# Layer 1 attention: gathers indexed from the slot table, later loads, and another order for the first tile

## The reference

```
x = x + tanh(g_xattn[0]) * L0_attention(layernorm(x), ctx)
x = x + tanh(g_ffn[0])   * L0_experts(layernorm(x))        # top 2 of 8
x = x + tanh(g_xattn[1]) * L1_attention(layernorm(x), ctx) # 16 heads, softmax over 77 keys
x = x + tanh(g_ffn[1])   * L1_ffn(layernorm(x))            # quantised weights and activations
```

## Time and profile before

| | us |
|---|---|
| median of 3 runs | 1357.1 (1356.96 to 1358.56) |
| the profiled execution, its own time | 1351.81 |
| its span, first to last instruction | 1350.1 |
| of it, layer 1 attention (901.36 to 1199.62) | 298 |
| mean granted TensorE clock | 0.949 |
| busy: TensorE / VectorE / ScalarE / GpSimd | 1194.5 / 982.7 / 811.0 / 549.5 |

### The profile page before, as it was taken

How to read it: one execution, slowest core, us unless ns; L and a number is a source line. 1 busy time by engine, 2 the same in 40 slices (tenths; PEclk the granted TensorE clock), 3 DMA queues, 4 the chain that set the end, 5 groups by cost and what they waited for, 6 DMA issues and landing times. The chain is left out here.

```text
span 1350.1 us, 26442 instructions
## 1 busy us (share of the span) xinstructions
PE 1194.5 (88%) x8487; PEld 899.4 (67%) x8533; DVE 982.7 (73%) x2135; ACT 811.0 (60%) x2405; POOL 549.5 (41%) x594
## 2 busy tenths in 40 slices
PE   4989898996986499999999999957999999959898
PEld 3878797884543277777777777734777777735475
DVE  4998889793554166666666667736888888859898
ACT  2555545452654256665566665516777777829898
POOL 4666757573204222221111112116888888710000
PEclk9999999998887599999999999988999999979999
DMA  3223233223774325333333332236224242100033
GB/s 116 64 94 94 72 94 93 70 79 95 254 217 117 134 59 138 112 114 118 115 112 118 122 115 95 69 112 180 63 64 139 64 139 64 41 12 1 32 98 122
DMA packets 124158, 135.30 MB, mean 100 GB/s; under 512 B 13838, under 2 KB 108740, under 8 KB 123908
## 3 DMA queue, kind: packets, MB, share of 16 engines
q1 hardware_dynamic: 116577, 114.81, 27.6%
q0 software_dynamic: 6816, 18.62, 5.1%
q10 hardware_dynamic: 642, 0.33, 0.1%
HBM read 84.43 MB, written 49.29 MB: 99 GB/s over the span
## 5 line engine op out<-in xcount | busy, mean ns | idle before, releaser
L1403 ACT ACTIVATE exp_h<-exp_ps_h,exp_b_now 128x256 f32<-128x256 f32 x312 | 128.8, 463 | 159.4 <-PE exp_ps_h L1343 156.2
L1343 PE MATMUL exp_ps_h<-exp_xhi,exp_w_now 128*128 128x256 bf16 x1248 | 214.8, 276 | 4.4 <-DVE exp_xlo L1433 4.4
L1788 ACT ACTIVATE a_z<-a_ps_sc,a_nmx 128x77 f32<-128x77 f32 x512 | 159.2, 368 | 56.2 <-DVE a_nmx L1889 56.2
L1343 PE MATMUL exp_ps_h<-exp_xlo,exp_w_now 128*128 128x256 bf16 x624 | 172.1, 276 | 0.0
L1510 DVE TENSOR_TENSOR exp_hlo<-exp_h,exp_hhi 128x512 bf16<-128x512 f32 x156 | 106.7, 691 | 80.4 <-ACT exp_hhi L1407 77.1
L1355 PE MATMUL exp_ps_y<-moe_w2s,exp_hhi 128*128 x585 | 139.2, 379 | 2.0
L1343 PEld LDWEIGHTS exp_ps_h<-exp_xhi,exp_w_now 128*128 128x128 bf16 x1248 | 123.5, 99 | 20.6 <-issue 5.0
L1788 ACT ACTIVATION_READ_ACCUMULATOR a_z<-a_ps_sc,a_nmx 128x1 f32 x512 | 127.9, 250 | 0.0
L1311 POOL COPY exp_at_now<-all_token_of 128x2 int32<-128x2 int32 x39 | 8.4, 216 | 288.7 <-PE exp_ps_x L1330 273.2
L1755 PE MATMUL a_ps_o<-a_v_now,a_phi 128*128 128x256 bf16 (+1 forms) x640 | 106.5, 272 | 15.4 <-DVE a_plo L1878 15.4
L1407 ACT ACTIVATE exp_hhi<-exp_h 128x512 bf16<-128x512 f32 x156 | 98.3, 630 | 4.9
(11 more groups left out here) (245 smaller groups left out, 2959.7 us busy)
## 6 DMA issues: line engine op xcount, KB each, us to landing
a_stage<-in_L_ffn_W_dram SPq DMA_DIRECT2D x64, 256.0 KB
y_slots<-exp_y SPq DMA_DIRECT2D x78, 128.0 KB
fold_k<-route_kst SPq DMA_DIRECT2D x16, 308.0 KB, 4.3
fold_v<-route_vst SPq DMA_DIRECT2D x16, 308.0 KB
exp_job_in<-fold_k SPq DMA_DIRECT2D x14, 352.0 KB, 3.4
exp_job_in<-fold_v SPq DMA_DIRECT2D x14, 352.0 KB, 3.3
a_x<-in_x_dram SPq DMA_DIRECT2D x32, 128.0 KB, 2.4
x<-a_xo SPq DMA_DIRECT2D x32, 128.0 KB, 1.7
```

What stands on the lines that cost most here:

```text
L1343: mm = pe.matmul(ps_h[:, i, f % 2 * SLOT_T:(f % 2 + 1) * SLOT_T], w1_now[:, v, k, hl, f * P:(f + 1) * P], xx[:, k, :], start=(q == 0), sto ...
L1403: ins = act.activation(h[:, f, :], ps_h[:, i, f % 2 * SLOT_T:(f % 2 + 1) * SLOT_T], ACT.Gelu_apprx_tanh, bias=b1_now[:, v, f:f + 1])
L1788: ins = act.activation(z[:, u, h * KEYS:(h + 1) * KEYS], ps_sc[:, j, (h - SB[j][0]) * KEYS:(h - SB[j][0] + 1) * KEYS], ACT.Exp, bias=nmx[: ...
```

## The change

The gather takes its index column directly from `C.slots`; the copy to `at_now` and the wait for it are gone. Before the loop SyncE now loads tiles 0 and 1, the biases, tiles 2 and 3, the keys of batch 0, waits until tile 0 is summed, and loads the values of batch 0. Keys and values of batch 1 are loaded in slot 4, and the feed-forward weights in slot 28. GpSimd runs `power(1)` before the scaling of the biases. VectorE normalises tile 0 and makes its low part before it turns to tile 1.

```diff
-        at_now = m.sb("at_now", [P, GR, TOPK], I32)
...
             for r in range(2):
                 load(r, r)
-            load_keys(0)
-            load_values(0)
             for i, bias in enumerate((bo, b_next)):
                 sp.dma_start(gbo[:, i, :], bias.partition_broadcast(P)).then_inc(bias_in, 16)
             for r in range(2, AHEAD):
                 load(r, r)
-            sp.dma_start(C.wi_q[:, :, :].rearrange("p k f -> p (k f)"), folded["wi_q"]).then_inc(s["w_loaded"], 16)
...
-            load_keys(1)
-            load_values(1)
+            load_keys(0)
+            sp.wait_ge(s["x2_done"], 1)
+            load_values(0)
...
-                if t == 4 and 1 <= b < B - 1:
-                    sp.wait_ge(s["scores_done"], NSB * b * TPB)
+                if t == 4 and b < B - 1:
+                    wait(sp, s["scores_done"], NSB * b * TPB)
                     load_keys(b + 1)
-                    sp.wait_ge(s["o_done"], b * TPB)
+                    wait(sp, s["o_done"], b * TPB)
                     load_values(b + 1)
+                if t == 4 and b == B - 1:
+                    load_ffn()
...
-                pool.tensor_copy(at_now[:, r, :].unsqueeze(2), C.slots[:, :, bass.ds(T, 1)]).then_inc(s["at_done"], 1)
-                copied = counted(pool, T + 1)
                 for c in range(TOPK):
                     pool.wait_ge(C.slots_stored[c], 16 * NST)
-                    if c == 0:
-                        pool.wait_ge(s["at_done"], copied)
                     pool.indirect_dma_start(out=yg[:, r, c, :], out_offset=None, in_=y_dram[:, :],
-                                            in_offset=bass.IndirectOffsetOnAxis(ap=at_now[:, r, c:c + 1].bitcast(U32), axis=0)
+                                            in_offset=bass.IndirectOffsetOnAxis(ap=C.slots[:, c, T:T + 1].bitcast(U32), axis=0)
...
             power(0, 0)
+            power(1, 1)
             pool.wait_ge(bias_in, 32)
...
-            power(1, 1)
...
                 ln_mean(T, T)
-            ln(0, 0, 0)
-            low_x(0, 0)
+                if T == 0:
+                    ln(0, 0, 0)
+                    low_x(0, 0)
```

More of the change, by code:

```diff
@@ L1576, in folded_attention @@
         v_loaded = [m.sem(f"v_loaded{i}") for i in range(2)]
-        names = ("at_done", "half_done", "x2_done", "stats_done", "mean_done", "veps_done", "rstd_done", "xn_done", "turned_x",
+        names = ("half_done", "x2_done", "stats_done", "mean_done", "veps_done", "rstd_done", "xn_done", "turned_x",
                  "xhi_done", "xlo_done", "w_loaded", "scores_done", "nmx_done", "exp_done",
@@ L1611, in load_values, with load_ffn @@
                     sp.dma_start(v_now[0:ROWS - whole, b % 2, hl, RCH - 1, :], rows[whole:ROWS, :]).then_inc(v_loaded[b % 2], 16)
+            def load_ffn():
+                sp.dma_start(C.wi_q[:, :, :].rearrange("p k f -> p (k f)"), folded["wi_q"]).then_inc(s["w_loaded"], 16)
+                sp.dma_start(C.wo_q[:, :, :].rearrange("p f d -> p (f d)"), folded["wo_q"]).then_inc(s["w_loaded"], 16)
+                with nc.allow_non_contiguous_dma(reason="a short bias, one element to a partition"):
+                    sp.dma_start(C.b_in[:, :], b_in.rearrange("(f p) -> p f", p=P)).then_inc(s["w_loaded"], 16)
             for r in range(2):
                 load(r, r)
-            load_keys(0)
-            load_values(0)
             for i, bias in enumerate((bo, b_next)):
@@ L1620, in _ @@
                 load(r, r)
-            sp.dma_start(C.wi_q[:, :, :].rearrange("p k f -> p (k f)"), folded["wi_q"]).then_inc(s["w_loaded"], 16)
-            sp.dma_start(C.wo_q[:, :, :].rearrange("p f d -> p (f d)"), folded["wo_q"]).then_inc(s["w_loaded"], 16)
-            with nc.allow_non_contiguous_dma(reason="a short bias, one element to a partition"):
-                sp.dma_start(C.b_in[:, :], b_in.rearrange("(f p) -> p f", p=P)).then_inc(s["w_loaded"], 16)
-            load_keys(1)
-            load_values(1)
+            load_keys(0)
+            sp.wait_ge(s["x2_done"], 1)
+            load_values(0)
             def slot(T, t, b):
```

## The result

The changed kernel takes 1339.26 us (median of 4 runs, 1337.17 to 1339.34), the kernel before 1357.03 beside it (4 runs, 1355.21 to 1358.56). The ratio is 0.9871, 95% interval 0.9856 to 0.9886. So it is faster, as forecast, but by 17.8 us and not by 23.7. The forecast 1333.5 is 5.8 us too low. The median lies just inside the upper end of the range (1339.5); set against the 1357.1 from which the forecast was worked out, 0.9871 gives 1339.6, just outside it.

A forecast was written before the change was run, and what follows sets the result against it. GpSimd, full despite idle gaps, was taken as the bound, with TensorE's 7.72 us slot next. Start 6.3 + rhythm 17.4 - loads 0.3 + tail 0.3 = 23.7 us off 1357.1, say 1333.5; range 1330.5 to 1339.5.

The forecast's parts named there:

- Rhythm: Slots 3 to 29: without the index copy GpSimd's slot falls to 7.34, below TensorE's 7.72; 17.4 us gained.
- three rivals of this part: GpSimd still the bound (1336, chance 0.20), VectorE and GpSimd interfering (1346.5, 0.07), TensorE's clock falling (slower, 0.02).
- The hold-up between the two engines: Rival: gather held up beside VectorE's two-input sum, slot 8.21, 10.5 us gained in all, 1346.5; chance 0.07 with a related case.
- clock rival: Fully busy TensorE granted 1.2 GHz, up to 7.7 us more per slot; 1360 with four such slots; chance 0.02.
- Later loads and tail: Loads moved to slots 4 and 28 cost 0.3 us together; the tail after slot 30 gains 0.3.
- Start: First tile alone first: 5.5 us gained at the first tiles, 0.8 from copies of slots 1 and 2; 6.3 at slot 3.
- the gather for tile 0: Stage start: issued at about 903.0, landing taken as 907.0, 2.8 to 5.8 us after issue being allowed.
- my own sign of being wrong: First scores were forecast at 912; coming after 913.5 would show the assumed landing wrong.
- GpSimd's three pairs of gathers: Stage start: without the copies they end at 909.2 instead of 911.3, bounds 908.9 and 910.6.
- The keys: Batch 0's 1.26 MB, issued at 904, are there by 908.6 at 271 GB/s, before the scores want them at 912.
- power(1): GpSimd at tile 1: left behind the bias scaling it would be 1.8 us later and cost about that.

The follow-up runs named there:

- x5: Changed kernel with the index copy put back, to a tile nothing reads, and no wait for it; ratio to the kernel before 0.9884.
- x2: The changed kernel run again unchanged for a second profile; 1335.2 us, ratio to the kernel before 0.9845.
- x4: Kernel before with only the index copy and its wait removed, gathers reading C.slots; loads and first tile as before; 1339.62 us.
- x3: Changed kernel with the two bias broadcasts issued behind the wait for tile 0's sum, ahead of the values; 1330.93 us.
- x10: Changed kernel with batch 0's keys held until tile 0's gathered rows land, and biases behind the wait for tile 0's sum; ratio to before 0.9823.
- x1: The kernel before run again unchanged for a second profile; 1355.5 us, ratio 0.9991.
- x7: Changed kernel with power(1) put back behind the scaling of the biases; ratio to the kernel before 0.9848.
- x11: x10 with the values of batch 0 also held until the biases have landed; 1333.35 us.
- x12: x11 with tile 2's gathers issued after power(0) on GpSimd; 1333.82 us, ratio to the kernel before 0.9844.

## Why the prediction was right in the rhythm and wrong at the start

**Rhythm: right.** GpSimd's slot fell below TensorE's, the bound became TensorE, and 27 slots of 7.718 gave 17.5 us against 17.4. Reading TensorE's floor from the last slots was good to 0.01. The three rivals of this part fell: GpSimd is not the bound, the gather is not held up by VectorE for long enough to matter, and the clock stayed at 1.00 at full load. The hold-up between the two engines was a sound rival all the same: put the copy back without its wait, and it costs 0.19 us per slot (x5). In the clock rival four slots at 7.7 more would have given 1364, not 1360.

**Later loads and tail: right.** VectorE's three waits for gathers, 1.43, 1.22 and 1.73, each in the slot behind loads of keys and values, are absorbed; TensorE waits in no such slot. The load in slot 28 makes nobody wait. Forecast -0.3, measured 0. Tail 0.45, forecast 0.3.

**Start: the step that failed.** Forecast 6.3 us at slot 3, measured 1.8 (after) and 3.1 (x2), mean 2.4. The step that failed is "the gather for tile 0 ... I take 907.0, since the values and half of the other loads are no longer in front of it". That is +5.65; it was +9.29 and +9.25, and my own sign of being wrong, scores after 913.5, came true. The gather took 7.4 us from its issue (911.06 to 918.45), outside the 2.8 to 5.8 that I allowed. I reasoned from the amount queued. Two things are shown in its place. Taking the values away brought nothing: with them in front and the broadcasts behind, the rows were used at +8.02 and +8.60, and at +8.18 without the copies (x4); without either in front it was +8.10 (x3); only holding the keys and tiles 2 and 3 as well brought them to +4.9 (x10). And the new order puts the broadcasts beside the gathers, which before stood behind the keys and values; that cost 1.15. The table gives the price of each load in front: +4.8 with tiles 0 and 1 only, +8.1 with tiles 2 and 3 and the keys too, +9.3 with the biases as well. How the 3.2 us between the first two divide between the keys and the tiles, no run tells. The rest of the chain held: GpSimd's three pairs of gathers ended at +7.85 (forecast +7.84), from the rows' use to the first normalisation it was 2.57 us (forecast 2.85), and to the scores 2.46 more (2.18). So the scores' shortfall, 3.7 us, is the landing's. The keys, forecast at +7.2, were there only at +14.3: I counted 271 GB/s from their issue on, and the engines moved 106 from 911 to 915.

**TensorE's clock at the start.** In the first slot the scores run at the lower level until the clock rises: 3.5 us after their start before, 5.5 after, 2.8 in x2. The first tile's scores took 4.83 us (917.95 to 922.78) before and 4.47 in x1, 5.83 (923.48 to 929.31) after and 4.47 in x2. Those 1.36 us cover the whole difference between after and x2 at slot 3 (1.27), and I had no term for it. It is chance between executions of one kernel, so a difference of about 1 us at slot 3 between two single profiles does not by itself rank two orders of the start.

**power(1).** Forecast to be worth 1.8 us in its new place; worth a few tenths at most (x7).

**From the stage to the time.** 6.3 + 17.4 - 0.3 + 0.3 = 23.7 became 2.4 + 17.5 + 0 + 0.45 = 20.3. I put the other 2.5 us, down to the 17.8 of the medians, to chance in the untouched stages; with x2 beside it the medians gave 21.0. How large that chance is the profiles show: from the stage's start to the program's end the changed kernel is 448.7 - 428.4 = 20.3 us faster, but its stage began 7.8 us later, and in the spans 1350.1 - 1337.6 = 12.5 is left. I had seen that the profiled run was 5.3 us under its median, and widened nothing for it. A range for the difference of two medians needs some 3 us on each side for that alone, by my estimate from 17.8 and 21.0 for one and the same change.

**Not settled:** which version is the best. From the stage's start x11 and x12 lead by 2.4 us over the changed kernel's mean, x3 by 1.6, but their times (1333.35, 1333.82, 1330.93 against 1335.2) lie within the spread of the untouched stages.

## What to carry to other kernels

Where an engine is full by the sum of its slot though it shows idle time, take the small instruction together with the wait behind it, and read the next bound from the last slots of the loop, where the old one has nothing to do. At the start of a stage, ask of the transfer that everything waits for which other transfers are in flight beside it, not only which are queued ahead; hold the big loads and the broadcasts until it has landed. Here that brought the first scores 2.8 us forward, and whether it shortens the whole program the times leave open. And when stages that the change does not touch vary by several us, measure the change from the start of its own stage.

## What was unexpected of the hardware

- A gather behind an ordinary GpSimd operation has a gap of 0.17 us, smaller than behind another gather (0.30). The 0.77 of before was the wait for the copy.
- Loads issued by SyncE slow a gather issued by GpSimd from a landing at +4.8 to one at +9.3. The Trainium skill (DMA: Bandwidth & Descriptors, "Issuing engines are not separate DMA queues") says that DMAs of all engines interleave on the same DMA engines; the runs agree and give that price.
- Two broadcasts of a 1 KB row to 128 partitions, issued first, halve what the DMA engines move in 8 us (98 and 218 GB/s against 191 and 372).
- A normalisation on VectorE of 0.41 us took 1.32 beside an addition on GpSimd that started 0.45 us after it (x5).
- Busy throughout for 208 us, TensorE kept its clock at 1.00. The one fall seen between the first scores and the last slots of any run (x12) came behind 3 us in which it was busy for 1.24, and the scores at the lower level took 1.7 us longer, about what the earlier start had won.
